# Moving the steps that prepare the next batch to other bursts, in the first stage of a four-stage transformer tower

## The reference

```python
h = emb + pe                                   # token embedding, 29 -> 128
x = layernorm(h)
Q, K, V = x @ Wq.T + bq, x @ Wk.T + bk, x @ Wv.T + bv
Q, K, V = (t.reshape(B * 8, L, 16) for t in (Q, K, V))   # 8 heads
attn = softmax(Q @ K^T * 16 ** -0.5)
out = (attn @ V).reshape(B, L, D) @ Wo.T + bo + x
h = h + layernorm(out) * gamma + beta
```

## Time and profile before

| | us |
|---|---|
| median of 3 runs | 1534.49 |
| lowest and highest run | 1532.92, 1535.9 |
| the profiled execution, own time | 1528.62 |
| its span, first to last instruction | 1526.8 |
| the first stage's exponentials, first to last start | 55.3 to 649.3 |
| distance of two batches' first exponentials, batches 1 to 6 | 75.5 to 77.0 |
| the last batch, which prepares no next one | 60.3 |

### The profile page before, as it was taken

The page is one execution under the profiler, slowest core; times in us unless marked ns, Lnnn a source line. Parts: engine busy times, 40 slices in busy tenths (PEclk is TensorE's granted clock), DMA queues, the critical chain, the costliest instruction groups (busy, mean ns, idle before and its releaser), DMA issues. The chain is left out here.

```text
span 1526.8 us, 26947 instructions
## 1 busy us (share of the span) xinstructions
PE 1202.5 (79%) x9465; PEld 804.9 (53%) x9465; DVE 928.9 (61%) x2492; ACT 993.9 (65%) x1348; POOL 578.6 (38%) x548
## 2 busy tenths in 40 slices
PE   3698898989898989915999994789871399999930
PEld 2344343434343434404788883677761288888820
DVE  5365868687768785541666665787752166666622
ACT  0487687868786869900989993454520399999920
POOL 3422333333333332230000001167775257777654
PEclk9599999999999999957999997788865599999975
DMA  3472737272727272212222200011111566777619
GB/s 94 95 186 70 165 91 168 87 169 86 170 86 170 82 169 83 84 29 73 94 79 88 83 28 11 1 35 45 48 46 47 216 222 233 233 242 246 230 52 300
DMA packets 108920, 180.88 MB, mean 118 GB/s; under 512 B 15867, under 2 KB 80854, under 8 KB 101742
## 3 DMA queue, kind: packets, MB, share of 16 engines
q1 hardware_dynamic: 81166, 129.62, 30.8%
q0 software_dynamic: 17344, 42.68, 8.3%
q10 hardware_dynamic: 10272, 6.82, 1.9%
HBM read 117.27 MB, written 63.12 MB: 118 GB/s over the span
## 5 line engine op out<-in xcount | busy, mean ns | idle before, releaser
L445 ACT ACTIVATE a_probs<-a_psS 128x1024 f32<-128x1024 f32 x512 | 483.1, 1042 | 119.2 <-PE a_psS L530 62.7
L964 DVE TENSOR_TENSOR f_g_lo<-f_g,f_g_hi 128x512 fp32r<-128x512 f32 x284 | 195.7, 690 | 162.4 <-ACT f_g L875 159.9
L542 PE MATMUL a_psO<-a_probs,a_v 128*32 128x256 f32 x4096 | 284.7, 397 | 0.3 <-ACT a_probs L445 0.3
L872 ACT ACTIVATE f_g_hi<-f_psH,f_w 128x512 fp32r<-128x512 f32 x284 | 198.8, 700 | 40.2 <-PE f_psH L71 38.0
L1757 POOL DMA_INDIRECT result<-f_out,f_idx x156 | 182.7, 1171 | 102.4 <-issue 60.0
L530 PE MATMUL a_psS<-a_qs,a_ks 50*128 50x512 f32 x1024 | 192.8, 455 | 19.2 <-ACT a_probs L445 9.7
L875 ACT ACTIVATE f_g<-f_psH,f_w 128x512 f32<-128x512 f32 x284 | 198.7, 700 | 0.0
L542 PEld LDWEIGHTS a_psO<-a_probs,a_v 128*32 128x32 f32 x4096 | 109.1, 111 | 137.0 <-issue 91.4
L530 PEld LDWEIGHTS a_psS<-a_qs,a_ks 50*128 50x128 f32 x1024 | 78.9, 190 | 121.0 <-ACT a_probs L445 67.5
L69 PE MATMUL f_psH<-f_x_hi,f_w 128*128 128x512 f32 x284 | 124.5, 438 | 5.1 <-DMA f_w<-experts 4.2
L1267 POOL DMA_INDIRECT queue<-all_row,all_idx x112 | 109.5, 978 | 32.9 <-issue 32.7
(11 more groups left out here) (294 smaller groups left out, 2120.7 us busy)
## 6 DMA issues: line engine op xcount, KB each, us to landing
f_w<-experts SPq DMA_DIRECT2D x55, 1026.5 KB, 5.3
experts<-a_split POOLq DMA_DIRECT2D x32, 512.0 KB, 4.4
f_rows<-queue SPq DMA_DIRECT2D x39, 260.0 KB, 5.3
qparts<-a_parts SPq DMA_DIRECT2D x16, 512.0 KB, 4.4
a_qs<-qparts SPq DMA_DIRECT2D x32, 256.0 KB, 4.8
kparts<-a_parts SPq DMA_DIRECT2D x14, 512.0 KB, 3.4
a_ks<-kparts SPq DMA_DIRECT2D x28, 256.0 KB, 6.7
a_qs<-qparts SPq DMA_DIRECT2D x32, 128.0 KB, 5.7
```

Of the source, the lines that this page charges most:

```text
L445: nc.scalar.activation(probs[u % NPR][:, :], psS[score_buffer(u)][:, :, :].rearrange("p a n -> p (a n)"), ACT.Exp).then_inc(exp_done, 1)
L542: last = nc.tensor.matmul(psO[32 * g:32 * g + 32, a * HALF:(a + 1) * HALF], v[par][:, 2 * hp + p, kt, :], probs[u % NPR][:, cols:cols + HA ...
L872: nc.scalar.activation(g_hi[i][:, n, :], psH[n][:, :], ACT.Gelu, bias=bias(m, n))
L964: nc.vector.tensor_tensor(g_lo[i][:, n, :], g[:, n, :], g_hi[i][:, n, :].bitcast(F32), ALU.subtract).then_inc(lo_done, 1)
```

## The change

Only the tables differ. Five of the twelve steps stand one burst earlier: T0, q0, T1, k1 and N1. Four `UPPER` pieces and three `SPLIT` pieces also stand elsewhere. No instruction is added or taken away.

```diff
-    STEPS = {1: ("E", 0), 3: ("E", 1), 5: ("T", 0), 7: ("q", 0), 9: ("k", 0), 11: ("T", 1), 13: ("q", 1), 15: ("k", 1),
-             17: ("N", 0), 19: ("N", 1), 27: ("v", 0), 29: ("v", 1)}
+    STEPS = {1: ("E", 0), 3: ("E", 1), 4: ("T", 0), 6: ("q", 0), 9: ("k", 0), 10: ("T", 1), 13: ("q", 1), 14: ("k", 1),
+             17: ("N", 0), 18: ("N", 1), 27: ("v", 0), 29: ("v", 1)}
-    SPLIT = {14: 0, 20: 1, 25: 2, 30: 3}
+    SPLIT = {12: 0, 19: 1, 28: 2, 30: 3}
-    UPPER = {2: ("moments", 0), 4: ("second", 0), 6: ("score", 0), 10: ("add_bias", 1), 12: ("normal", 1), 18: ("moments", 1), 23: ("second", 1),
+    UPPER = {2: ("moments", 0), 4: ("second", 0), 5: ("score", 0), 11: ("add_bias", 1), 12: ("normal", 1), 20: ("moments", 1), 22: ("second", 1),
              25: ("score", 1)}
```

## The result

The changed kernel takes 1607.9 us (median of 4 runs, 1599.7 to 1611.8) against 1533.7 for the kernel before (1531.7 to 1535.9). The ratio is 1.048, 95% interval 1.043 to 1.053: 74 us slower. The profiled execution took 1611.3, with a span of 1609.5. It lies 82.7 us above the profiled execution of before (1528.6), so the two traces differ by 8.5 more than the medians do. The forecast was 1592.6 in its working and 1592 on its last line, with a range of 1567 to 1613.

A forecast was written before the change was run, and what follows sets the result against it. ScalarE's exponentials set the pace without preparation; preparing batches added PE's step work and waits. Boundary 34.3, its low clock 7, end of batch 7 6.9 and middle 9.9 sum to 58.1, on 1534.5 giving 1592.6 us; range 1567 to 1613.

The forecast's parts named there:

- The bound, and the waits that go: PE's waits at the projections of bursts 16 and 8 and the q products, 39.8 us over six batches, were the target.
- T0 and bursts 4 to 9: T0 waits 1.2 us, burst 8's projection 0.3, its weighing waits for the transpose; burst 9 starts 1.5 us later.
- Bursts 9 to 17: k1 waits 3.0 us for psA, burst 16's weighing 2.1; burst 17 starts at 333.65, before it was 332.80.
- The boundary: Bursts 28 to 0: the fourth split piece waits for a late load; PE waits 4.9 us at 7 boundaries, 34.3 us.
- the end of batch 7: The same late-load chain without steps delays the last transpose by 6.9 us (5.7 to 9).
- The step with the landing: The late load, issued behind GpSimd's three operations and the store, lands 4.2 us later.
- the low clock: PE at 1.2 GHz behind waits: 1.0 us per boundary, 7 us in all, and 0.8 a batch in the middle.
- the middle: Bursts 4 to 17: 0.85 us a batch plus 0.8 of low clock, 1.65 over batches 1 to 6, 9.9 us.
- The first: Rival: the projection waits go and nothing takes their place, so faster, 1485 us; chance 0.05.
- The second: Rival: the load lands in time and only the middle gets worse, 1544 us; chance 0.05.
- The fourth: Rival: larger loss, loads at 6 us and low clock in full at each wait, 1619 us; chance 0.07.

The follow-up runs named there:

- the run with the sums first: Kernel before with SPLIT in 17, 21, 25, 30 and SP's sums stored and loaded before the next batch's second q and k loads: 1517.4 us.
- the run with 20 products: Changed kernel plus 20 unread 128x128 products on TensorE ahead of burst 0's projection in batches 1 to 7: 1595.8 us.

## Why the prediction was right, point by point

**The bound, and the waits that go.** Right. The three waits of the earlier trace rows, 39.8 us, fell to 1.3 us. As forecast, nothing was gained by it.

**T0 and bursts 4 to 9.** T0's wait: 1.2 forecast, 1.14 measured. The projection of burst 8: 0.3 and 0.23. The weighing behind it for the transpose: a start at 310.15 against a projection ended at 308.0, 2.1, and 2.10 measured.

**Bursts 9 to 17.** k1's wait was put at 3.0 with the split at 0.42 + 1.62 taken from batch 7; it is 3.11, with 0.42 + 1.60. The wait of burst 16 was put at 2.1 and was 1.57 in batch 3, from 0.26 to 2.77 elsewhere. It is the remainder of VectorE's time after PE's, so whatever slows PE before it shortens it.

**The boundary.** The wait was put at 4.9 a time; it was 4.84, 4.28, 4.25, 4.40, 4.36, 5.78 and 4.34, mean 4.6. At the end of batch 7 the forecast was 6.9; from the weighing of burst 0 of that batch to the last transpose it is 65.2 us against 58.2, 7.0 more. The step with the landing was right too: 4.2 us assumed, 4.05 in batch 3. The rule in the Trainium skill, "DMA: Bandwidth & Descriptors", section "Anatomy of one DMA — SWDGE (gpsimd) path", gives an estimate of 2.6 for it. By the measured 4.05 it is too low for the way from issue to landing of a load issued right behind a store.

**The term that was mis-sized: the low clock.** It was taken as 1.0 us at the boundary and 0.8 in the middle, from one row, as if each batch kept its single fall of 1.56. In batches 1 to 6 it is much more. If the clock stands at one of its two levels, a mean of 0.97 is 6% of the time at half clock, an estimate of 27 of 457 us; 0.88 is 24%, 126 of 527 us. PE's busy time grew by 39.1 us for it, 6.5 a batch. Of this 16.4 us, 2.7 a batch, stand in bursts 0 to 3 behind the boundary, where 1.0 was forecast. The other 22.7, 3.8 a batch, stand in the middle, where the forecast had 0.8 less the old 1.56. The forecast for the same six batches had 1.0 + 0.8 - 1.56 = 0.2 a batch of slower work and 4.9 + 0.85 + 1.56 = 7.3 of new idle time. Measured are 6.5 and 5.2, so the idle part was too high by 2.1 and the slow part too low by 6.3. Before, a batch had waits of 0.7 to 3.3 us and mostly one fall of the clock. Now it has waits of some 4.6, 1.1, 2.1, 3 and up to 2.8 us, and the clock is low behind most of them: behind the boundary for two bursts, in burst 9, in bursts 15 to 17, and in some batches in burst 22.

**The parts.** The boundary with the end of batch 7 was forecast at 34.3 + 7 + 6.9 = 48.2 and is 55 (1607.9 against 1552.9); the middle at 9.9 and is 19. Both are short for the same reason: the run with the third split piece back in 25 has only the middle, and there 22.5 of the 25.6 us that its six batches are longer are slower work.

**The range.** That 1607.9 lies inside it is luck in part. Its upper end was made of a boundary wait of 5.9 us and a middle of 3 us a batch, with at most 1.56 us of slow work in it. The wait came out shorter than forecast, and the slow work, 3.8 us a batch in the middle alone, filled the place. The ends given for the two parts, 4.3 to 5.9 and 0 to 3, also make 1578.5 to 1607.7 when they are added up, and not the 1573 and 1610 that the prediction has.

**The rivals.** None happened as written. The first rested on the waits of the earlier trace rows being the cause; the run with the split pieces at 17 and 21 shows that the largest was for the most part the split piece's (3.2 us became 0.35), and that a late `ctxT` stood close behind it. The second, with the load in time, is what the run with the third split piece in 25 makes: 1552.9 where it had 1544, again for the clock. The fourth was nearest, at 1619: its low clock in full at each wait came, and its loads of 6 us did not.

## What to carry to other kernels

Where an in-order engine serves several others, moving one of its pieces takes the wait from one client to the next: list, for every piece moved, who waits for what now stands behind it, and where the data of the next such piece is loaded. Two pieces joined by a store and a load need the whole round trip between them; here five bursts of 1.8 us worked (0.7 us of waits for the load in all) and two did not. Beside busy DMA engines four or five bursts still left 28.7 to 47.1 us of such waits. Before a wait is taken away, look for what is ready only just in time behind it, since that is the next limit. And price a wait with the slow work behind it: here the low clock cost more than the added idle time.

## What the runs showed of the hardware

The granted clock was not expected to cost more than the idle time that brings it. A wait of 2.6 us after 2.9 us of products was followed by a weighing of 1.93 us in place of 1.07, and one of 0.96 us after 4.7 us of products was not. Nor was one of 2.02 us, in batch 1 of the run with 20 products. But in the changed kernel each of the four waits of 2.10 us at burst 8 was followed by a weighing of 1.93 or 1.94 one burst later, and in batch 2 of the run with 20 products the same wait was not. So the length of one wait does not tell the clock behind it. In batches 1 to 6 of the changed kernel 31 us more idle time came with 39 us more busy time for the same instructions. Filling the wait with unread products gave 12 us back (1607.9 to 1595.8).

Loads of `a_raw` took 4.6 us from issue to landing in the changed kernel (median, 3.9 to 9.4). What else the DMA engines carry goes with it: in batch 3 of the run with the sums first two of them took 7.7 and 8.4 us, with the DMA engines busy for 0.94 and 0.91 of that time, and the late load of batch 3 in the changed kernel took 4.0 at 0.57.
